# A set of fillers taken out of TensorE's instruction stream: threshold WARM from 0.8 to 0.0

## The chip, the core and the metric

The kernel runs on one core of a Trainium2 chip. The metric is the time of one execution on the device, in microseconds (us); the median of several executions is compared. Engines are written as in the profile: PE is TensorE (PEld its weight loads), DVE is VectorE, ACT is ScalarE, POOL is GpSimd, and SP issues most of the DMAs.

## What is computed

The input is x of 4 batches x 1024 tokens x 256 channels. Two layers follow, each with a layer norm ahead and a residual around it:

```python
x = x + attn(layernorm(x))        # theta, phi (64 wide), g (256): (theta phi^T / 16) g, no softmax
x = x + ffn(layernorm(x))
# ffn: h = rmsnorm(x); q, k, v = h @ wqkv.T    (16 heads, 4 kv heads, 16 wide), rope on q and k
#      x = x + softmax(causal(q k^T / 4)) v @ wo.T
#      h = rmsnorm(x); router: softmax(h @ gate_w.T), the best 2 of 8 experts per token
#      out = sum over the chosen experts of (silu(h w1^T) * (h w3^T)) w2^T * weight
```

## The kernel before

The first attention has no softmax, so the kernel forms it per batch as a 256 x 256 product ("gram", L2016, from the normalized tokens `xn`, then "square", L2029) and applies it to the tokens ("x1", L2038). "xnT" (L2009) and "hT" (L2045) are transposes of 128 x 128 tiles by TensorE. "k_mm", "q1_mm", "q2_mm" (L2071) and "v" (L2056) are the projections of the second attention; "max" (L2085, L2088, L2092, L2093) computes scores only for their row maxima, which DVE takes (L1881, L1883); "maxT" (L2098) transposes the maxima; "score" (L2105) computes the scores, ACT takes their exponential (L1360), POOL masks, and "pv" (L2119) multiplies with v. "wo" (L2126) closes a batch. The rows of each batch are then sorted by expert and go through "blockT", "up", "gatedT", "down" (L2139, L2152/L2167, L2174, L2189).

Nothing is ordered by hand. `plan()` simulates the five engines in Python, with an assumed duration for each step (`WORK_OF`), and writes out one fixed list of steps per engine. Each engine then works through its list in order, and waits for semaphores where a step needs another engine's result or a bank of PSUM (7 banks go around among the steps; the 8th is that of "pv").

The change touches one helper in this plan, `keep_warm(until)`. It is called whenever the planner is about to place a step on PE that starts at the planned time `until`. While the steps placed within the last `WINDOW` (3.4) us of planned time ahead of `until` add up to no more than `WARM` times `WINDOW`, and a planned gap is left, it puts a filler ("warm") into PE's list: one product of the 128 x 128 identity with itself, in f32, planned at `WARM_TOOK` (0.22 us), into a PSUM bank that is free in the plan. A filler's result is read by nobody. In the kernel it is

```python
if stage == "warm":
    q.wait_ge("load_eye", 16)
    e.matmul(bk[:, 0:P], ident, ident, start=True, stop=True)
```

Of the kernel before, what the change touches and what calls it, by code (L numbers as in the profile page):

```python
# [242 lines left out]
           "blockT", "up", "gatedT", "down")  # L243

WARM, WINDOW, WARM_TOOK, WARM_FROM = 0.8, 3.4, 0.22, 5.0

SPACING = 3.5

# [1984 lines left out]
```

## Time and profile before

| | us |
|---|---|
| median of three executions | 1090.14 |
| lowest, highest | 1088.01, 1091.58 |
| span of the profiled execution, first to last instruction | 1087.9 |
| TensorE busy in the span | 1042.4 |

### The profile page before, as it was taken

What the parts mean: (1) busy time and instruction counts of PE and PEld (TensorE: products, weight loads), DVE (VectorE), ACT (ScalarE), POOL (GpSimd) and SP (SyncE); (2) the same over time, 40 slices, a digit from 0 to 9 for tenths busy, and PEclk for the clock granted to TensorE, in tenths of its full rate; (3) what the DMA queues carried; (4) which work ended last, traced back from release to release, by engine and by line L of the source; (5) the groups of instructions that cost most, each with busy time, mean ns of one, the idle gap of its engine ahead of it and who ended that gap; (6) DMA issues with size and microseconds to landing.
All of it is one profiled execution on the core that took longest, in us unless ns stands there. A gap on an engine that the chain in (4) does not pass through costs nothing.

```text
span 1087.9 us, 19824 instructions
## 1 busy us (share of the span) xinstructions
PE 1042.4 (96%) x6630; PEld 619.5 (57%) x6630; DVE 763.2 (70%) x1811; ACT 581.1 (53%) x1124; POOL 421.9 (39%) x493
## 2 busy tenths in 40 slices
PE   7999999999999999999999999999999999999996
PEld 6765335564435333354333533456667986679996
DVE  4699999768788897788886699243485555555552
ACT  3563566646677887747666566641432244453320
POOL 2020232625643134521434512555637833344332
PEclk9999999999999999999999999999999999999999
DMA  6334113322324656723342511233434432222322
GB/s 192 124 94 122 51 49 106 93 76 77 100 75 140 187 175 193 216 78 99 105 126 85 140 55 37 65 75 74 103 83 98 99 62 38 45 36 40 50 43 27
DMA packets 85732, 101.50 MB, mean 93 GB/s; under 512 B 17632, under 2 KB 73312, under 8 KB 85632
## 3 DMA queue, kind: packets, MB, share of 16 engines
q1 hardware_dynamic: 70752, 80.60, 25.7%
q0 software_dynamic: 14880, 19.64, 9.5%
q8 instruction: 55, 0.90, 0.3%
q14 instruction: 45, 0.37, 0.1%
HBM read 55.76 MB, written 41.14 MB: 89 GB/s over the span
## 4 chain that ended last, share of the span: by engine, by line
PE 70%; DVE 19%; issue 4%; ACT 4%; POOL 1%; DMA 1%; SPq 0%; POOLq 0%; DVEq 0%; ACTq 0%
PE psum L2167 12%; PE psum L2189 9%; PE psum L2119 9%; PE psum L2152 8%; PE psum L2105 7%; DVE psum L1881 7%; PE psum L2085 4%; DVE mx L1883 3%; PE psum L2161 3%; PE psum L2071 3%; PE psum L2126 2%; PE psum L2088 2%; ACT probs_mem L1360 2%; PE psum L2092 2%; PE psum L2038 2%
## 5 line engine op out<-in xcount | busy, mean ns | idle before, releaser
L1360 ACT ACTIVATE probs_mem<-psum 128x512 f32<-128x512 f32 (+1 forms) x464 | 233.6, 585 | 103.3 <-PE psum L2105 98.6
L1881 DVE CUSTOM_DVE_ANT_1 psum<-psum,masking 128x640 f32<-128x640 f32 (+3 forms) x256 | 256.9, 1046 | 31.1 <-PE psum L2088 28.2
L2105 PE MATMUL psum<-stack_mem 98*128 98x512 bf16 (+3 forms) x768 | 170.9, 327 | 6.0 <-ACT probs_mem L1360 2.4
L1259 POOL DMA_INDIRECT out<-yout,labels x68 | 108.9, 1602 | 164.7 <-DVE yout L1961 78.1
L1200 POOL TENSOR_SCALAR_AFFINE_SELECT probs_mem<-probs_mem 128x512 f32<-128x512 f32 x104 | 67.7, 653 | 237.4 <-ACT probs_mem L1360 237.1
L2105 PEld LDWEIGHTS psum<-stack_mem 98*128 98x128 bf16 x768 | 65.0, 97 | 104.5 <-ACT probs_mem L1360 21.5
L1385 ACT ACTIVATE gated<-psum 128x512 f32<-128x512 f32 x68 | 40.6, 597 | 150.9 <-PE psum L2152 68.9
L2119 PE MATMUL psum<-probs_mem,v 128*17 128x512 f32 (+3 forms) x1152 | 116.0, 490 | 0.6 <-ACT heads_out L1367 0.2
L2189 PE MATMUL psum<-w_mem,gated 128*128 x480 | 114.4, 381 | 0.0
L1883 DVE TENSOR_REDUCE mx<-psum 128x4 f32<-128x512 f32 (+2 forms) x96 | 96.6, 1040 | 19.5 <-PE psum L2093 11.8
L2085 PE MATMUL psum<-stack_mem 96*128 96x512 bf16 x256 | 94.8, 383 | 8.6 <-DVE mx L1881 5.1
L2189 PEld LDWEIGHTS psum<-w_mem,gated 128*128 128x128 f32 x480 | 88.1, 190 | 24.6 <-issue 14.6
L1360 ACT ACTIVATE gated<-psum 128x512 f32<-128x512 f32 x144 | 78.9, 617 | 37.8 <-PE psum L2105 37.0
L2152 PE MATMUL psum<-w_mem,blockT 128*128 x200 | 95.2, 599 | 2.7 <-ACT probs_mem L1360 1.7
L1955 DVE TENSOR_TENSOR gated<-psum,gated 128x512 f32<-128x512 f32 x68 | 47.0, 692 | 48.2 <-PE psum L2167 20.6
L1951 DVE SCALAR_TENSOR_TENSOR gated<-gated,psum 128x512 f32<-128x512 f32 x68 | 46.6, 686 | 46.5 <-ACT gated L1385 45.0
L2088 PE MATMUL psum<-stack_mem 96*128 96x128 bf16 (+3 forms) x256 | 76.3, 298 | 0.0
L1230 POOL DMA_INDIRECT routed<-hrow,route_mem x64 | 64.1, 1002 | 29.2 <-DVE hrow L1940 16.1
L2167 PE MATMUL psum<-blockT,probs_mem 128*128 128x128 f32 x576 | 70.2, 275 | 0.0
L2167 PEld LDWEIGHTS psum<-blockT,probs_mem 128*128 128x128 f32 x576 | 68.6, 192 | 0.9
L2085 PEld LDWEIGHTS psum<-stack_mem 96*128 96x128 bf16 x256 | 24.7, 96 | 74.7 <-DVE mx L1881 33.5
L2167 PE MATMUL psum<-blockT,stack_mem 128*128 128x128 f32 x544 | 66.2, 275 | 0.0
(243 smaller groups left out, 1770.1 us busy)
## 6 DMA issues: line engine op xcount, KB each, us to landing
block<-routed SPq DMA_DIRECT2D x68, 129.0 KB
w_mem<-in_w13T SPq DMA_DIRECT2D x16, 512.0 KB, 4.4
qk_parts<-w_mem SPq DMA_DIRECT2D x16, 384.0 KB, 2.6
stack_mem<-qk_parts SPq DMA_DIRECT2D x32, 192.0 KB, 3.0
w_mem<-in_x SPq DMA_DIRECT2D x8, 512.0 KB, 5.3
out<-w_mem SPq DMA_DIRECT2D x8, 512.0 KB, 4.1
x_late<-out SPq DMA_DIRECT2D x8, 512.0 KB, 5.0
stack_mem<-qk_parts SPq DMA_DIRECT2D x32, 128.0 KB, 2.6
```

What stands on the lines that cost most here:

```text
L1200: e.affine_select(pb[:, :, q0:q0 + P], pb[:, :, q0:q0 + P], [[0, GRP], [1, P]], ALU.is_ge, 0.0, base=0, channel_multiplier=-1).then_inc(se ...
L1259: e.indirect_dma_start(out_rows, bass.IndirectOffsetOnAxis(ap=to, axis=0), youts[w % NYOUT], None, bounds_check=NBATCH * SEQ - 1, oob_is_e ...
L1360: e.activation(probs[probs_of(m)][:, hh:hh + n, q0:CH], grid(turn[step][0][:, 0:n * (CH - q0)], n), ACT.Exp, scale=float(HD) ** -0.5).then ...
L1881: e.tensor_tensor_reduce(keys, keys, masked(w), 1.0, -3e38, ALU.add, ALU.max, to).then_inc(sem["max"], 1)
L1883: e.tensor_reduce(to, took, AX.X, ALU.max).then_inc(sem["max"], 1)
L2085: e.matmul(bk[:, 0:CH], rows_of, s[0:STACK, 0, GRP, :], start=True, stop=True)
L2088: m = e.matmul(to, rows_of, s[0:STACK, r, GRP, 0:w], start=True, stop=True)
L2105: m = e.matmul(bk[:, i * (CH - q0):(i + 1) * (CH - q0)], s[0:STACK + NMAX, kt // TPR, GRP, kt % TPR * P:(kt % TPR + 1) * P], s[0:STACK + N ...
L2119: m = e.matmul(pv_bank[32 * hh:32 * hh + HD + 1, q0:CH], v1[:, b, kt, g, :], pb[:, hh, q0:CH], start=(kt == KEYS[r][0]), stop=(kt == KEYS[ ...
L2152: m = e.matmul(bk, blockT[w % 2][:, k], w13_s[:, k, bass.ds(offset[w] + half * FFN, FFN)], start=(k == 0), stop=(k == KD - 1))
L2167: m = e.matmul(bk[:, c * P:(c + 1) * P], slots[copies_of(w)[0] % NSLOT][:, k, half * FFN + c * P:half * FFN + (c + 1) * P], blockT[w % 2][ ...
L2189: m = e.matmul(bk[:, 0:D], rowsT[:, k * P:(k + 1) * P], w2_mem[:, bass.ds(offset[w] + k * D, D)], start=(k == 0), stop=(k == KF - 1))
```

## The change

`WARM` becomes 0.0. The loop of `keep_warm` then stops as soon as anything was placed within the last 3.4 us of planned time. It still adds a filler where nothing was.

```diff
-WARM, WINDOW, WARM_TOOK, WARM_FROM = 0.8, 3.4, 0.22, 5.0
+WARM, WINDOW, WARM_TOOK, WARM_FROM = 0.0, 3.4, 0.22, 5.0
```

PE's list has 87 fillers before and 8 after. The 79 that are gone stood: 12 of 15 ahead of the first batch's gram, 16 of 21 around the first hT (17, 1 and 3 before, 5 after), 10 of 10 in the second batch's projections, and 41 of 41 later (11 at 346 to 352 us, 1 at 438 us, 28 from 466 to 496 us, 1 at 628 us of the profiled execution). The order of all other steps is the same on all five engines; some waits for a bank now stand on the next step in the place of the filler.

The first place is PE's start. L2001 is the product of the weights theta and phi ("pair"), L1997 a filler, L2016 the gram of the first batch; the words in brackets are the semaphores that the instruction waits for.

```order
 L2001 MATMUL psum<-w_mem 128x256
 L1997 MATMUL psum<-ident 128x128 [waits load_eye]
-L1997 MATMUL psum<-ident 128x128 x3
-L1997 MATMUL psum<-ident 128x128 [waits pair_out]
-L1997 MATMUL psum<-ident 128x128 x10
+L1997 MATMUL psum<-ident 128x128 x2
 L2016 MATMUL psum<-w_mem 128x256 [waits xn]
```

The gram moves up by 12 fillers; its own waits for `xn` stay.

The second place is PE at the first batch's hT (L2045, which waits for `h` from ACT); L2071 is the projection for the keys, whose list of waits names `hT_out` (ACT's copy of the transposes).

```order
 L1997 MATMUL psum<-ident 128x128 [waits xnT_out]
-L1997 MATMUL psum<-ident 128x128 x14
+L1997 MATMUL psum<-ident 128x128 x2
 L2045 MATMUL psum<-ident,w_mem 128x128 [waits h]
 L2045 MATMUL psum<-ident,w_mem 128x128 x3
-L1997 MATMUL psum<-ident 128x128
 L2045 MATMUL psum<-ident,w_mem 128x128 [waits h,x1]
 L2045 MATMUL psum<-ident,w_mem 128x128 x3
-L1997 MATMUL psum<-ident 128x128 x3
 L2071 MATMUL psum<-w_mem 64x512 [waits wqkv,hT_out,x1]
```

Of the 17 fillers ahead of the transposes 5 stay (the piece shows the last three, two more stand ahead of it), and the one between the transposes and the three behind them go.

The third place is PE around 492 to 498 us of the trace: L2092 and L2093 end a pair of maxima, L2119 is pv.

```order
-L1997 MATMUL psum<-ident 128x128
-L1997 MATMUL psum<-ident 128x128 [waits max]
-L1997 MATMUL psum<-ident 128x128 x7
 L2119 MATMUL psum<-probs_mem,v 17x128 [waits mask]
 L2119 MATMUL psum<-probs_mem,v 17x128 x3
-L1997 MATMUL psum<-ident 128x128 [waits max]
-L1997 MATMUL psum<-ident 128x128 x2
 L2119 MATMUL psum<-probs_mem,v 17x512 [waits pv_out,mask]
 L2119 MATMUL psum<-probs_mem,v 17x512 x3
 L2119 MATMUL psum<-gated,v 17x512 x4
```

The two groups of pv move up to the end of the maxima; the nine and the three fillers ahead of them go.

## Rows read from the trace of the kernel before

**Rows 1.** Busy time of each engine over the span (the page's first part).

```profile
PE 1042.4 (96%) x6630; PEld 619.5 (57%) x6630; DVE 763.2 (70%) x1811; ACT 581.1 (53%) x1124; POOL 421.9 (39%) x493
```

**Rows 2.** All fillers of the kernel (groups by line: busy us, mean ns, idle before).

```profile
L1997 PE MATMUL psum<-ident 128*128 128x128 f32 x174 | 26.5, 297 | 0.1
```

**Rows 3.** Stretches: busy us (xcount) of PE, PEld, DVE, ACT, POOL, PEclk, DMA, GB/s.

```profile
60.00:105.00 45.00, 42.76 (x247) 29.79 (x247) 42.69 (x125) 24.64 (x48) 5.99 (x7) 1.00 0.43 130
466.00:496.00 30.00, 27.48 (x171) 18.18 (x172) 28.36 (x65) 12.08 (x34) 7.06 (x15) 1.00 0.23 67
540.00:1079.00 539.00, 532.25 (x3327) 356.15 (x3319) 319.12 (x683) 234.34 (x416) 243.61 (x275) 1.00 0.32 70
```

**Rows 4.** Timeline of PE, 7.9 to 22.4 us (start, us, engine, line, tiles).

```profile
7.94 2.07 PE L2001 MATMUL psum<-w_mem 64*128 64x256 f32 x4 [7.94 <-DMA w_mem<-in_wphi]
9.94 5.66 PE L1997 MATMUL psum<-ident 128*128 128x128 f32 x30
15.44 7.07 PE L2016 MATMUL psum<-w_mem 128*128 128x256 f32 x32
22.34 1.04 PE L2009 MATMUL psum<-ident,w_mem 128*128 128x128 f32 x8
```

**Rows 5.** Fillers by their source line, in 9 to 14 us and in 36 to 41 us.

```profile
L1997 PE MATMUL psum<-ident x19: 421/421/580, 9.9 to 13.9; 128*128 128x128 f32 x19
...
L1997 PE MATMUL psum<-ident x34: 275/275/343, 36.5 to 40.2; 128*128 128x128 f32 x34
```

**Rows 6.** Timeline of ACT, 10 to 16 us.

```profile
10.04 0.60 ACT L1270 ACTIVATE w_mem<-psum 128x512 f32<-128x512 f32 x1 [7.96 <-PE psum L2001]
10.54 2.07 ACT L1278 ACTIVATE w_mem<-w_mem,rt 128x256 f32<-128x256 f32 x4
12.96 2.08 ACT L1278 ACTIVATE w_mem<-w_mem,rt 128x256 f32<-128x256 f32 x4 [0.36 <-DVE rt L1458]
```

**Rows 7.** Chain that ended last, 9 to 31 us (start us, us, what).

```profile
10.01 5.59 PE psum L1997 x30
15.60 6.91 PE psum L2016 x32
...
30.61 0.69 DVE w_mem L1822
```

**Rows 8.** Timeline of PE, 36 to 44 us.

```profile
36.46 4.03 PE L1997 MATMUL psum<-ident 128*128 128x128 f32 x34
40.72 0.66 PE L2045 MATMUL psum<-ident,w_mem 128*128 128x128 f32 x4 [0.23 <-ACT w_mem L1285]
...
43.20 1.90 PE L2071 MATMUL psum<-w_mem 128*64 128x512 f32 x4
```

**Rows 9.** Timeline of PE where the next fillers stand, 71 to 76 us.

```profile
71.75 1.28 PE L1997 MATMUL psum<-ident 128*128 128x128 f32 x10
73.60 1.99 PE L2038 MATMUL psum<-w_mem 128*128 128x256 f32 x8 [0.57 <-ACT w_mem L1325]
```

**Rows 10.** Chain, 438 us: the one filler that it holds in mid-kernel.

```profile
438.35 0.42 PE psum L1997 x2
```

**Rows 11.** Timeline of PE, 492 to 500 us.

```profile
492.13 2.31 PE L1997 MATMUL psum<-ident 128*128 128x128 f32 x18
...
494.81 0.94 PE L1997 MATMUL psum<-ident 128*128 128x128 f32 x6
...
499.61 0.39 PE L2105 MATMUL psum<-stack_mem 98*128 98x512 bf16 x1 [0.72 <-ACT probs_mem L1360]
```

**Rows 12.** Timeline of ACT, 494 to 500 us.

```profile
495.87 3.31 ACT L1299 ACTIVATE hrow<-hrow,rstd 128x256 f32<-128x256 f32 x8 [0.42 <-DVE rstd L1444]
499.08 1.22 ACT L1360 ACTIVATE probs_mem<-psum 128x384 f32<-128x384 f32 x3
```

**Rows 13.** Stretches after PE's last matmul (columns as in rows 3).

```profile
1078.40:1082.40 4.00, 0.04 (x1) 0.00 (x0) 0.48 (x1) 0.00 (x0) 1.21 (x1) 1.00 0.24 27
1082.40:1083.00 0.60, 0.00 (x0) 0.00 (x0) 0.00 (x0) 0.00 (x0) 0.15 (x1) 0.69 0.00 0
```

## The prediction

> **What bounds the kernel now.** I read the page first. TensorE (PE) is busy 1042.4 us of the span of 1087.9 [rows 1], so whatever stands in PE's list and isn't needed is suspect. All fillers together are 174 records, two for each of 87, with 26.5 us of busy time [rows 2]. That is the most that their removal could be worth if PE never waited for another engine; it would be 2.4% of the span. So the question for each group of fillers is whether PE had something else to do in that time.
>
> The stretches of the span answer most of it [rows 3]. From 60 to 105 us DVE is busy 42.69 of 45 us, from 466 to 496 us 28.36 of 30. In both, and in the shorter one at 346 to 352 us, PE waits for DVE to empty banks, and the fillers fill that wait. From 540 us to PE's end PE is busy 532.25 of 539 us and DVE 319.12: there PE is the bound, but only one filler (at 628 us) stands there. What comes earlier in the kernel and is saved for good is therefore kept to the end, since that last stretch only moves.
>
> Then I read the start as a timeline and as the chain that ended last. PE begins with the pair product at 7.94 us, runs 15 fillers (30 records) from 9.94 to 15.44, and then the gram, 32 records from 15.44 to 22.34 [rows 4]. The chain of what ended last goes through these fillers and the gram, and on to DVE's first x1 at 30.61 us [rows 7]. So the fillers at the start are on the path. What the gram needs is ready earlier: ACT normalizes the first four tiles from 10.54 us on, at about 0.5 us each, and the other four from 12.96 us [rows 6].
>
> **The change, part by part.**
>
> *The first 12 fillers.* A record's median duration is 421 ns up to 13.9 us, and 275 ns in the group at 36 us [rows 5]: until about 14.2 us TensorE ran at its lower level (1.2 GHz), and then at 2.4 GHz, after some 6.3 us in which it had run without a pause since 7.94. From the starts, the 20 records before 14.26 took 0.216 us each ((14.26 - 9.94) / 20), and the last ten 0.118 (1.18 us to 15.44). The gram's records take (22.34 - 15.44) / 32 = 0.216 us each at the high level; at the low one I take twice that, 0.432. The pair product's records of as many columns took 0.50 ((9.94 - 7.94) / 4), which is my upper bound. In the changed kernel three fillers stay: 6 x 0.216 = 1.3 us, so the gram can start at 11.24. The first tile is there by then: 10.54 + 0.52 = 11.06, with some latency 11.3. While the clock is low a gram step (four records) takes 1.73 us and ACT delivers a tile every 0.5, the fifth at about 13.5, so `xn` is never late again. From 11.3 to 14.26 seven records run, the other 25 take 25 x 0.216 = 5.4 us, and the gram ends at 19.7 where it ended at 22.34: **2.65 us earlier**. With 0.50 us for a slow record it is 2.4. If the clock rises one microsecond later than before, this loses 0.5 us, so I hold 1.2 to 3.6 us for this term.
>
> After the gram come PE and ACT alone, then DVE at 30.61 with the x1 of the first batch. DVE's work ahead of that is done long before: in the chain it is PE that DVE waits for there [rows 7].
>
> *The 16 fillers around the first hT.* The 17 ran from 36.46 to 40.49 us, and the transposes then still waited 0.23 us for ACT's h; the keys' projection starts at 43.20 behind ACT's copy [rows 8]. Nothing that PE did there held anything up: **0 us**. But here the cover goes. Five fillers end about 1.2 us after 36.46, at 37.6, and PE then stands for 3.1 us until 40.72; of the 5.6 us to 43.20 it works only for the two groups of transposes. If TensorE's clock falls in there, the projections start at the low level. The only fall in this trace is at the end: after PE's last matmul at 1078.4 the granted clock is still 1.00 up to 1082.4 and 0.69 on the mean over the next 0.6 us [rows 13], so it fell some 4.2 us after the last work. That is longer than the 3.1 us without any work, and shorter than the 5.6 with a little. From the row alone I call it open, and take no fall.
>
> The Trainium skill, "TensorE: Matmul & The Clock Gate", section "Why this matters for your kernels", speaks against the change here: it warns that a gap in TensorE's work of about the length opened here, between bursts of matmuls, takes the clock back to half. By that rule the sum would be near zero (the first rival); by the row it is the 2.65 us.
>
> *The 10 fillers of the second batch.* The five from 71.75 us are followed by a wait of 0.57 us for ACT [rows 9], and those near 85 us stand in the stretch in which DVE is full [rows 3]: 0. PE then idles 1.9 us at the first, shorter than anything above.
>
> *The 41 later.* 39 lie in the stretches in which DVE is full: 0. The one at 438 us is in the chain with 0.42 us [rows 10], but some 20 us later PE waits for ACT and POOL anyhow, and the one at 628 us has a wait for DVE behind it: 0 to 0.4 us together, taken as 0. The largest group is the 9 and 3 fillers at 492 and 494.8 us (2.31 and 0.94 us) [rows 11]. Without them PE is 3.1 us ahead, since the masks of that pv are long done. But ACT, in order, first has the eight steps that wait for DVE's rstd until 495.87, and begins the exponentials only at 499.08 [rows 12]; PE waits for the first of them until 499.61 either way [rows 11]. DVE is without a gap ahead of rstd. So the lead turns into a wait of 3.8 us: 0 us, and a second place at which the clock may fall, of the same kind.
>
> **Sum.** 1087.9 - 2.65 = 1085.2 us of span. The median of the timed runs lies 2.2 us above the profiled span; I keep that: **1087.5 us**.
>
> **Rivals.**
>
> *The clock falls around the first hT and the gain is given back.* For: 5.6 us with PE nearly idle. Against: two groups of transposes break them, and the only row of a fall shows 4.2 us of no work at all. Price: the low level lasts, as at the start, some 6.3 us of running, here from 43.2 to 49.5, in which PE gets half as far: 3.1 us lost. These projections feed DVE (it waits for them), so it is on the path. Sum: 1090.14 - 2.65 + 3.1 = 1090.6; with a fall late in the gap or a quick return 1089.
>
> *Slower by over 0.3%: the clock stays low for long after that gap.* Each microsecond at the low level from 43.2 us on costs half a microsecond, and 2.65 us are in hand. It ends above 1093.4 only if the low level lasts more than (3.3 + 2.65) x 2 = 11.9 us; at 15 us it gives 1090.14 - 2.65 + 7.5 = 1095. Against: the clock came up after 6.3 us at the start, and PE runs almost without pause after 43.2.
>
> *The lead of PE at 495 us counts.* If the exponentials aren't what PE needs there, 3.1 us more are kept: 1090.14 - 2.65 - 3.1 = 1084.4. For: it is PE that bounds the rest. Against: the wait for ACT that stands in the row today.
>
> *The fillers at the start cost nothing* (something else holds the gram or its followers, a table or a weight that lands late): 1090.
>
> **How the numbers follow.** Gain at the start kept, 0.48: 1087.5, its own range 1085.5 to 1089. Clock falls at the first hT, 0.30: 1089 to 1091. No gain for another reason, 0.06. Clock low for long, 0.06: 1095. Lead at 495 us kept, 0.10: 1084.4. The range of 1084.5 to 1091.5 leaves out the long low clock and the lower half of the last case, and a little at either end. A measurement of this kernel tells about 0.3% (3.3 us) from no change, so faster starts below 1086.9. The likeliest case is 0.6 us short of that; the three runs of before lie within 3.6 us, so I give it about a third of the likeliest case (0.16) and nearly all of the lead (0.09): 0.25 faster. Slower has the long low clock and a small share of the short one: 0.08. The same: 0.67.
>
> **What would show it.** Right: the gram ends near 19.7 us, DVE's first x1 starts near 28.0, records behind 40 us keep 275 ns (128 columns), PE waits 3 us or more for ACT near 493 us, and the span is 2 to 3 us shorter. Wrong: a granted clock under 1.00, or projections of the first batch with doubled durations at 40 to 50 us; a clock that rises later than some 14 us at the start; a first x1 that is not earlier.

## The result and the profile after

The changed kernel takes 1094.39 us in the median of 8 executions (1092.34 to 1099.18), the kernel before 1089.2 in 8 (1087.93 to 1091.58). The ratio is 1.0049 (95% interval 1.0036 to 1.0063): some 5.3 us slower. The forecast was 1087.5 us with a range of 1084.5 to 1091.5: the time lies outside it, and the gain did not come. The profiled execution has a span of 1092.5 us, with TensorE busy for 1032.0 us (10.4 less than in [rows 1]) and a mean granted clock of 0.988 (0.998 before). So PE was busy 10 us less, and the kernel became slower.

The page of the changed kernel shows PE's busy share and the granted clock in 40 equal slices of the span, in tenths.

```profile
PE   7899899999998999988999999999999999999996
...
PEclk9899999999999999998999999999999999999999
```

The second slice (27 to 55 us) has a clock of 8 tenths. PE has five slices of 8 where the page of before has none. The timeline of PE shows the start and the first hT (start, us, line, tiles).

```profile
9.66 1.65 PE L1997 MATMUL psum<-ident 128*128 128x128 f32 x6
11.10 7.54 PE L2016 MATMUL psum<-w_mem 128*128 128x256 f32 x32
18.48 1.04 PE L2009 MATMUL psum<-ident,w_mem 128*128 128x128 f32 x8
...
32.59 1.35 PE L1997 MATMUL psum<-ident 128*128 128x128 f32 x10
36.85 2.16 PE L2045 MATMUL psum<-ident,w_mem 128*128 128x128 f32 x8 [2.91 <-ACT w_mem L1285]
39.74 5.31 PE L2071 MATMUL psum<-w_mem 128*64 128x512 f32 x8 [0.73 <-issue]
```

Three fillers (6 records) are left at 9.66 us, the gram runs from 11.10 to 18.48 us (15.44 to 22.34 in [rows 4]). Five fillers (10 records) stand at 32.59; then PE waits 2.91 us for ACT's h. The eight transpose records that follow take 2.16 us, and the eight of the keys' projection 5.31 us. In the kernel before such eight took 3.82:

```profile
43.20 3.82 PE L2071 MATMUL psum<-w_mem 128*64 128x512 f32 x8
```

These are the stretches around each fall of the clock in the changed kernel (columns as in [rows 3]).

```profile
32.60:35.90 3.30, 1.34 (x12) 1.15 (x10) 3.27 (x30) 1.04 (x3) 0.00 (x0) 1.00 0.71 240
36.00:42.70 6.70, 5.12 (x12) 2.18 (x12) 2.48 (x15) 6.48 (x14) 0.00 (x0) 0.50 0.60 190
42.80:46.00 3.20, 3.20 (x16) 1.93 (x16) 2.73 (x4) 0.75 (x2) 0.00 (x0) 1.00 0.89 282
...
349.00:353.30 4.30, 2.66 (x17) 0.68 (x17) 4.30 (x13) 3.79 (x10) 0.00 (x0) 1.00 0.59 164
353.40:356.70 3.30, 3.30 (x18) 0.58 (x11) 3.13 (x11) 0.47 (x2) 0.00 (x0) 0.50 1.13 339
...
466.00:469.40 3.40, 1.38 (x7) 0.50 (x7) 2.85 (x7) 3.40 (x9) 0.72 (x1) 1.00 0.52 133
469.50:472.80 3.30, 3.30 (x9) 1.67 (x9) 1.58 (x4) 2.74 (x7) 0.28 (x1) 0.50 0.13 41
496.50:500.10 3.60, 1.98 (x15) 0.60 (x7) 3.12 (x15) 2.69 (x7) 0.00 (x0) 1.00 0.14 29
500.20:506.90 6.70, 5.69 (x21) 1.85 (x22) 3.48 (x12) 5.49 (x14) 1.27 (x2) 0.50 0.65 174
```

The clock is granted at 0.50 (1.2 GHz) from 35.9 to 42.8 us, from 353.4 to 356.8, from 469.4 to 472.8 and from 500.1 to 507.0. Ahead of each, PE worked only part of the time: 1.34 of 3.30 us, 2.66 of 4.30, 1.38 of 3.40, 1.98 of 3.60. Each of the four is a place that had fillers before, and PE is busy during most of each low stretch, so it pays for it.

How DVE's lead went is read from its timeline at five steps, in the kernel before:

```profile
45.15 0.68 DVE L1842 TENSOR_TENSOR w_mem<-psum,w_mem 64x512 f32<-64x512 f32 x1 [2.31 <-PE psum L2071]
...
337.83 1.23 DVE L1883 TENSOR_REDUCE mx<-psum 128x2 f32<-128x1024 f32 x1 [0.32 <-PE psum L2093]
...
359.14 1.23 DVE L1881 CUSTOM_DVE_ANT_1 psum<-psum,masking 128x1024 f32<-128x1024 f32 x1
...
470.26 0.43 DVE L1905 TENSOR_TENSOR hrow<-psum,hrow 128x264 f32<-128x264 f32 x1
...
506.36 0.23 DVE L1932 COPY route_mem<-psum 128x64 f32<-128x64 f32 x1
```

and at the same steps in the changed kernel, with the first x1 ahead of them:

```profile
26.74 0.69 DVE L1822 TENSOR_TENSOR w_mem<-psum,w_mem 128x512 f32<-128x512 f32 x1 [4.24 <-PE psum L2038]
...
43.18 0.68 DVE L1842 TENSOR_TENSOR w_mem<-psum,w_mem 64x512 f32<-64x512 f32 x1 [4.22 <-PE psum L2071]
...
336.86 1.23 DVE L1883 TENSOR_REDUCE mx<-psum 128x2 f32<-128x1024 f32 x1 [0.32 <-PE psum L2093]
...
359.64 1.23 DVE L1881 CUSTOM_DVE_ANT_1 psum<-psum,masking 128x1024 f32<-128x1024 f32 x1 [1.55 <-PE psum L2088]
...
472.01 0.43 DVE L1905 TENSOR_TENSOR hrow<-psum,hrow 128x264 f32<-128x264 f32 x1 [0.98 <-PE psum L2126]
...
510.05 0.23 DVE L1932 COPY route_mem<-psum 128x64 f32<-128x64 f32 x1 [0.91 <-PE psum L2134]
```

The first x1 starts at 26.74 us where it was 30.61 [rows 7]: 3.87 us ahead. It is 1.97 ahead at the keys' projection (43.18 for 45.15), 0.97 ahead at a step before the second fall (336.86 for 337.83), 0.50 behind after the second fall (359.64 for 359.14), 1.75 behind after the third (472.01 for 470.26), 3.69 behind after the fourth (510.05 for 506.36), and the span is 4.6 us longer. The loss comes in steps, and each of the four falls has one: 1.90, 1.47, 1.25 and 1.94 us. Another 1.0 us goes between the first two falls, with no fall beside it. All of it goes at one place: PE waits 1.21 us for a DMA in the changed kernel, and the same step of the kernel before (at 117.75 us) has no wait for a DMA.

```profile
116.81 1.45 PE L2105 MATMUL psum<-stack_mem 98*128 98x512 bf16 x5 [1.21 <-DMA stack_mem<-mneg_parts]
```

The last 0.9 us (3.69 behind, then 4.6) are lost after 510 us, where the clock does not fall before PE's last matmul.

PE around 495 us, in the changed kernel:

```profile
493.65 0.41 PE L2119 MATMUL psum<-probs_mem,v 128*17 128x128 f32 x8
495.26 1.05 PE L2119 MATMUL psum<-probs_mem,v 128*17 128x512 f32 x8 [1.20 <-ACT heads_out L1367]
...
498.10 0.38 PE L2105 MATMUL psum<-stack_mem 98*128 98x512 bf16 x1
501.13 1.29 PE L2105 MATMUL psum<-stack_mem 98*128 98x512 bf16 x2 [2.66 <-ACT probs_mem L1360]
```

Without its twelve fillers PE doesn't run ahead: the second group of pv waits 1.20 us for ACT's copy of the first, and the scores wait 2.66 us for the exponentials, 3.86 us together.

### The profile page after: what moved, and what is told of

Its sections match the earlier page's. It is cut to its first block, busy times and chain, and to the rows that moved or that the text cites. A ratio compares the mean times of both kernels' runs of the same rounds, so it can differ in the third digit from the quotient of the medians.

```text
span 1092.5 us, 19511 instructions
## 1 busy us (share of the span) xinstructions
PE 1032.0 (94%) x6472; PEld 601.6 (55%) x6472; DVE 762.1 (70%) x1811; ACT 581.1 (53%) x1124; POOL 422.7 (39%) x493
## 4 chain that ended last, share of the span: by engine, by line
PE 64%; DVE 20%; DMA 6%; issue 5%; ACT 4%; POOL 1%; SPq 0%; POOLq 0%; DVEq 0%
PE psum L2119 9%; PE psum L2152 8%; PE psum L2167 8%; PE psum L2189 8%; DVE psum L1881 7%; PE psum L2105 7%; DMA out<-yout,labels 5%; PE psum L2085 4%; DVE mx L1883 3%; PE psum L2161 3%; PE psum L2071 3%; PE psum L2126 2%; ACT probs_mem L1360 2%; PE psum L2088 2%; PE psum L2038 2%
## 5 line engine op out<-in xcount | busy, mean ns | idle before, releaser
L2119 PE MATMUL psum<-probs_mem,v 128*17 128x512 f32 (+3 forms) x1152 | 117.3, 495 | 1.8 <-ACT heads_out L1367 1.4
L1883 DVE TENSOR_REDUCE mx<-psum 128x4 f32<-128x512 f32 (+2 forms) x96 | 96.5, 1040 | 19.5 <-PE psum L2093 14.3
L1961 DVE TENSOR_SCALAR yout<-psum,labels 128x256 f32<-128x256 f32 x68 | 32.8, 482 | 53.5 <-PE psum L2189 31.3
```

Of the source, the lines that this page charges most:

```text
L1883: e.tensor_reduce(to, took, AX.X, ALU.max).then_inc(sem["max"], 1)
L2119: m = e.matmul(pv_bank[32 * hh:32 * hh + HD + 1, q0:CH], v1[:, b, kt, g, :], pb[:, hh, q0:CH], start=(kt == KEYS[r][0]), stop=(kt == KEYS[ ...
```

## The experiments

Each kernel was timed in rounds beside the kernel before on the same chip. "At 0.997" counts the executions whose mean granted clock was 0.997 or more; the last column is the range of that mean. A low stretch of 7 us takes 0.003 off it. The fall behind PE's last matmul [rows 13] is in every mean. One execution of each kernel is profiled: the eight profiles with a mean of 0.997 or more (that of the kernel before among them) have no fall ahead of PE's last matmul, the nine with 0.995 or less have one to five. The kernel before itself was at 0.997 in 87 of the 121 executions beside these experiments: 14 of 19 beside e1 to e4, 16 of 29 beside e5, e6, e7 and e9, 23 of 29 beside e8, e10 and e11, 12 of 15 beside e12, and 22 of 29 beside e13 to e15.

| kernel | median us | before, us | ratio (95%) | at 0.997 | mean clock |
|---|---|---|---|---|---|
| changed kernel | 1094.39 | 1089.2 | 1.0049 (1.0036 to 1.0063) | 0 of 8 | 0.986 to 0.991 |
| e1_start: without the 12 | 1087.19 | 1090.25 | 0.9977 (0.9962 to 0.9992) | 5 of 7 | 0.995 to 0.998 |
| e2_hT: without the 16 | 1096.3 | 1090.25 | 1.0047 (1.0033 to 1.0062) | 0 of 5 | 0.990 to 0.993 |
| e3_346: without the 11 | 1091.58 | 1090.25 | 1.0012 (1.0 to 1.0023) | 3 of 12 | 0.994 to 0.997 |
| e4_466: without the 28 | 1094.72 | 1090.25 | 1.0048 (1.0033 to 1.0064) | 0 of 6 | 0.989 to 0.995 |
| e5_others: without the other 12 | 1088.63 | 1088.93 | 1.0 (0.9987 to 1.0012) | 10 of 12 | 0.994 to 0.998 |
| e6_transposes | 1090.71 | 1088.93 | 1.0016 (1.0002 to 1.003) | 5 of 12 | 0.994 to 0.998 |
| e7_half: without 14 of the 28 | 1091.61 | 1088.93 | 1.002 (1.0009 to 1.0031) | 2 of 12 | 0.993 to 0.997 |
| e9_start_kept | 1098.71 | 1088.93 | 1.0084 (1.0071 to 1.0097) | 0 of 6 | 0.984 to 0.987 |
| e8_early | 1086.78 | 1088.51 | 0.9983 (0.9973 to 0.9993) | 6 of 12 | 0.993 to 0.998 |
| e10_more | 1087.02 | 1088.51 | 0.9988 (0.9979 to 0.9996) | 11 of 11 | 0.997 to 0.998 |
| e11_hT_kept | 1090.06 | 1088.51 | 1.0017 (1.0005 to 1.003) | 0 of 12 | 0.986 to 0.995 |
| e12_early_more | 1090.34 | 1089.09 | 1.0011 (1.0002 to 1.002) | 2 of 11 | 0.991 to 0.997 |
| e13_250 | 1091.97 | 1091.3 | 1.0004 (0.9994 to 1.0014) | 10 of 12 | 0.996 to 0.998 |
| e14_early_250 | 1089.3 | 1091.3 | 0.9982 (0.9971 to 0.9994) | 7 of 12 | 0.995 to 0.997 |
| e15_hT_250 | 1095.6 | 1091.3 | 1.0034 (1.0022 to 1.0045) | 0 of 12 | 0.992 to 0.995 |

Gains and losses in us below are (ratio - 1) x 1090.

### One group at a time

Fillers were taken out of the finished plan of the kernel before, by their number in it, so that every other step stayed as it was:

```diff
+        gone = {*range(3, 15)}
+        orders["PE"] = [s for s in orders["PE"] if s[0] != "warm" or s[1] not in gone]
+        steps = [s for s in steps if s[0] != "warm" or s[1] not in gone]
```

**e1_start** is this diff: fillers 3 to 14, ahead of the first gram. (The added lines move all line numbers behind them: a filler is L2000 here, the gram L2019.)

> The kernel before without the 12 fillers ahead of the first gram; the other 67 that the change takes away stay. Clock theory (the fillers later in the list kept TensorE's clock up, and the change lost time because it fell at four places): no fall of the clock here, so the gain at the start stays to the end. The changed kernel had DVE's first x1 3.87 us earlier than before, of which some 0.4 us was there before the first matmul: 3 to 3.9 us faster than before. Rival (an early lead is lost in later waits anyhow): DVE's first x1 earlier by as much, and the whole within 1 us of before.

Measured: ratio 0.9977, 2.5 us faster. Its timeline of PE:

```profile
9.70 1.65 PE L2000 MATMUL psum<-ident 128*128 128x128 f32 x6
11.14 8.24 PE L2019 MATMUL psum<-w_mem 128*128 128x256 f32 x32
19.22 1.04 PE L2012 MATMUL psum<-ident,w_mem 128*128 128x128 f32 x8
```

The gram ends at 19.22 us, 3.1 us before that of [rows 4]; the mean clock over the profiled execution is 0.997, with no fall before PE's last matmul. The lead stays: the span of the profile is 1084.9 us, 3.0 shorter than before. The median's gain is a little under the 3 to 3.9 us of the clock theory, but the interval (0.9 to 4.1 us) takes in both that range and, just, the 1 us of the rival.

**e2_hT**: `gone = {*range(20, 36)}`, the 16 around the first hT.

> The kernel before without the 16 fillers around the first hT. Clock theory: the granted clock falls to 0.50 between 38 and 48 us and the keys' projection (8 records) takes 5.3 us and not 3.8; slower than before by about 1.9 us, what DVE's lead shrank by there in the changed kernel. Rival (the lead shrank there because of an issue or a wait, not the clock): the clock stays at 1.00, and the time is within 0.5 us of before or later by the same 1.9.

Measured: 1.0047, 5.1 us slower, more than either theory said. The clock did fall at the hT, from 41.9 to 48.7 us, and so later against the steps than in the changed kernel. There 0.9 us of the low stretch fell into PE's wait for ACT; here it covers the keys' projection almost from end to end:

```profile
43.21 6.51 PE L2074 MATMUL psum<-w_mem 128*64 128x512 f32 x8 [0.73 <-issue]
```

That is 6.51 us where the changed kernel took 5.31 and the kernel before 3.82. The profile had a second fall where no filler had been taken:

```profile
253.50:256.90 3.40, 2.32 (x23) 2.06 (x21) 3.33 (x6) 2.34 (x5) 3.18 (x4) 1.00 0.31 69
257.00:263.70 6.70, 6.04 (x28) 2.26 (x26) 3.95 (x5) 3.64 (x10) 2.24 (x2) 0.50 0.07 15
```

The kernel before has the same lull at the same steps, and the clock held there in its profile (the stretch that begins with the same four scores, 2.31 us of work in 3.4):

```profile
250.60:254.00 3.40, 2.31 (x21) 2.01 (x20) 3.33 (x6) 2.48 (x6) 3.18 (x4) 1.00 0.29 65
```

So the same stretch of instructions can end with a fall or without one. Its cause in e2 was open; e15 below takes it up.

**e3_346**: `gone = {*range(46, 57)}`, the 11 at 346 to 352 us.

> The kernel before without the 11 fillers at 346 to 352 us. Clock theory: the clock falls for 3.4 us or more near 350 to 360 us, 1.5 to 2 us slower than before, unless the fall depends on where the kernel's steps lie in the chip's own time, in which case some executions show it and others don't. Rival (fillers there are free to remove, as predicted): 0.

Measured: 1.0012, 1.3 us slower. Three of the twelve executions had a mean clock of 0.997 and a median of 1089.42 us, the nine others 0.995 or less and 1092.86. One program, two outcomes, 3.4 us apart, told apart by the clock: the "sometimes" of the expectation. The profile is one of the nine:

```profile
346.00:349.70 3.70, 2.43 (x12) 0.87 (x12) 3.59 (x13) 3.08 (x6) 0.63 (x1) 1.00 0.27 71
349.80:356.60 6.80, 6.59 (x31) 1.33 (x33) 6.77 (x19) 4.80 (x12) 0.00 (x0) 0.50 0.76 231
```

**e4_466**: `gone = {*range(58, 86)}`, the 28 at 466 to 496 us.

> The kernel before without the 28 fillers at 466 to 496 us. Clock theory: falls near 470 and near 500 us, 3 us slower (1.2 and 1.9 us of DVE's lead went at these places in the changed kernel). Rival (as predicted, PE's lead only becomes a wait): 0.

Measured: 1.0048, 5.2 us slower; no execution kept its clock. Falls at 486.4 and 500.0 us, the first elsewhere than in the changed kernel:

```profile
483.00:486.40 3.40, 1.59 (x7) 0.89 (x7) 3.32 (x8) 0.55 (x3) 0.72 (x1) 1.00 0.14 46
486.50:489.80 3.30, 3.30 (x21) 2.37 (x20) 2.75 (x8) 0.36 (x2) 0.53 (x1) 0.50 0.14 30
496.60:500.00 3.40, 1.00 (x5) 0.53 (x6) 2.73 (x12) 3.40 (x10) 0.15 (x1) 1.00 0.29 57
500.10:503.40 3.30, 3.30 (x16) 0.82 (x15) 1.25 (x3) 2.61 (x6) 1.02 (x2) 0.50 0.84 286
```

**e5_others**: `gone = {*range(36, 46), 57, 86}`. These are the ten in the second batch's projections and the ones at 438 and 628 us.

> The kernel before without the 12 fillers that the clock never seemed to need: 10 in the second batch's projections, those at 438 and 628 us. Both theories: the time of before within 1 us, 0.4 us faster at best. If the granted clock falls somewhere all the same, then small gaps matter too, and it is 1 to 3 us slower.

Measured: 1.0 (0.9987 to 1.0012), with 10 of 12 executions at 0.997: while the other fillers stand, taking these twelve out changes neither the clock nor the time by anything that shows.

**e9_start_kept** is the changed kernel with its first 12 put back: `gone = {*range(20, 87)}`.

> The changed kernel with its 12 fillers ahead of the first gram put back. If the parts add up, it is slower than the changed kernel by what these 12 cost alone (2.5 us): ratio to before 1.0072, 7.8 us slower than before. If the single costs of the three later groups simply add, 5.1 + 1.3 + 5.2 = 11.6 us slower than before.

Measured: 1.0084, 9.2 us slower than before, between the two sums. The start's 12 are worth 3.8 us against the changed kernel (1.0084 - 1.0049; the two intervals leave room for 2.5), and the later groups together cost less than the sum of their single costs (11.6 us). The profile has five falls ahead of PE's last matmul, at 42.4, 100.4, 353.0, 492.9 and 506.6 us. The one at 100.4 us lies behind the ten fillers of the second batch, which are gone here too, and DVE falls 1.2 us further back there. So the ten are not without use in every kernel, though e5 by itself shows none.

**e11_hT_kept** is the changed kernel with the 16 around the hT put back: `gone = {*range(3, 15), *range(36, 87)}`.

> The changed kernel with its 16 fillers around the first hT put back. If they alone are worth what their absence cost the kernel before, it is 5 us faster than the changed kernel: about the time of before, ratio 1.000. By DVE's lead in the changed kernel alone, which shrank by 1.9 us there, 2 us faster than the changed kernel: ratio 1.003. No fall of the clock before 340 us in either case.

Measured: 1.0017. Against the changed kernel these 16 give back (1.0049 - 1.0017) x 1090 = 3.5 us: between the 2 us of DVE's lead and the 5 us of e2. As expected the profile has no fall ahead of 340 us; it has two, at 485.1 and 498.7 us, and none at 346 to 352 us, whose fillers are gone as well.

### How much filling, and of what kind

**e7_half**: `gone = {*range(59, 86, 2)}`.

> The kernel before without every second one of the 28 fillers at 466 to 496 us (14 go). Clock theory: with half of the fillers the stretch of PE without work before the exponentials is some 1.6 us longer, not 3 to 4, so the clock holds in most executions: within 1.5 us of before. If only the full set holds it: 5 us slower, as without all 28. Rival without a clock: half of what all 28 cost, 2.6 us.

Measured: 1.002, 2.2 us slower; 2 of 12 executions at 0.997. The time alone fits the rival's 2.6 us too. The clocks speak against it: 10 of 12 executions were at 0.996 or less, where the kernel before had 13 of 29 beside it. So half of the fillers do not hold the clock in most executions, as the clock theory had expected. The one profile has a single fall, from 469.1 to 472.5 us, where e4 had two.

**e6_transposes**: in the branch of "warm",

```diff
+                    if 20 <= at[0] < 36:
+                        e.transpose(bk[:, 0:P], ident, ident)
+                    else:
-                    e.matmul(bk[:, 0:P], ident, ident, start=True, stop=True)
+                        e.matmul(bk[:, 0:P], ident, ident, start=True, stop=True)
```

> The kernel before with all 87 fillers, but the 16 around the first hT are transposes of the identity by TensorE in the place of plain products: the same count, tile, place and length of work. If the clock theory holds and a transpose counts as work like any other, nothing changes (within 1 us of before, no fall near 40 us). If a transpose does not hold the clock up, as the Trainium skill has it, the granted clock falls near 40 us and the time is that of the kernel without these 16, about 5 us slower than before. If what the missing fillers cost is not the clock but something in the list, this kernel is like before in any case and shows no fall.

Measured: 1.0016 (1.7 us), 5 of 12 executions at 0.997. The expectation had one thing wrong, as the timeline shows:

```profile
35.52 1.35 PE L2003 MATMUL psum<-ident 128*128 128x128 f32 x10
36.71 1.47 PE L2001 MATMUL psum<-ident 128*128 128x128 f32 x12
39.78 0.66 PE L2051 MATMUL psum<-ident,w_mem 128*128 128x128 f32 x4 [1.60 <-ACT w_mem L1288]
```

Twelve transposes are 12 records in 1.47 us, where twelve products are 24 in twice that: a transpose of this tile shows as one record, and PE was left with a wait of 1.60 us. So it was not the same length of work. Still, without any of the 16 no execution of 5 was at 0.997 (e2), and with half the work as transposes 5 of 12 were (16 of 29 of the kernel before beside it); the profile has a mean clock of 0.998 and no fall near 40 us. Transposes do something for the clock. Whether as much as products of the same length was not measured. The Trainium skill, "TensorE: Matmul & The Clock Gate", section "Part 4: PE-mode transpose", says that they don't count as work in the same way; these runs don't decide it.

**e8_early**, with `gone = {*range(6, 15)}` and

```diff
+            q.wait_ge("set", 1)
+            for _ in range(14):
+                e.matmul(bank[6][:, 0:P], pad[:, 0:P], pad[:, 0:P], start=True, stop=True)
             for step in orders["PE"]:
```

> The kernel before with 14 fillers more at its very start (products of a cleared 128 x 128 tile, about 6 us of TensorE at the low clock, while it waits for the first weights until 7.9 us), and only 6 of the 15 ahead of the first gram. Clock theory: the clock is up by about 8 us in the place of 12 to 15, so the pair product and the gram run at the high level: the gram ends near 18.2 us (22.3 before, 18.5 and 19.2 without the 12 fillers), some 4 us faster than before and 1 to 1.5 faster than the kernel that only leaves the 12 out. If products of a cleared tile don't raise the clock, or if it comes up only after the loads, nothing is won over that kernel: 2.5 us faster than before.

Measured: 0.9983. The profile shows what was meant:

```profile
1.18 5.51 PE L1994 MATMUL psum<-left_rows 128*128 128x128 f32 x28 [1.18 <-POOL left_rows L1151]
7.83 1.13 PE L2007 MATMUL psum<-w_mem 64*128 64x256 f32 x4 [1.14 <-DMA w_mem<-in_wphi]
8.89 1.60 PE L2003 MATMUL psum<-ident 128*128 128x128 f32 x12
10.93 7.17 PE L2022 MATMUL psum<-w_mem 128*128 128x256 f32 x32 [0.43 <-ACT w_mem L1281]
17.94 1.04 PE L2015 MATMUL psum<-ident,w_mem 128*128 128x128 f32 x8
```

The 28 records run from 1.18 us; the pair product then takes 1.13 us (2.07 in [rows 4]) and the gram ends at 17.94. Products of a cleared tile raise the clock. Yet the ratio is no better than e1's, and not the 4 us that were expected: half of the executions had a mean clock of 0.995 or less (1087.5 us in the median), the other half 0.997 or more (1085.3).

**e10_more**: WARM at 1.0, and at most 3 fillers ahead of the first gram.

> WARM raised to 1.0 in the place of 0.0, and no more than 3 fillers ahead of the first gram: 14 more fillers than the kernel before has in its other places. The kernel before shows a mean clock under 0.996 in a third of its executions. If those are falls at stalls that its 72 other fillers don't quite cover, fewer executions show one here, and the median is 3 us under before, 0.5 better than the kernel without the 12 alone; if fillers by now stand in the way of work, it is slower than that kernel by up to 14 x 0.24 = 3.3 us.

Measured: 0.9988 (0.9979 to 0.9996); all 11 executions at 0.997 or more, where the kernel before had 34 of 121 at 0.996 or less. With more fillers no execution shows a fall. But the median is 1.3 us under before and not 3, and not below e1's; whether the added fillers stand in the way of work somewhere was not measured.

**e12_early_more** joins e8 and e10.

> Both together: the 14 early products and 6 fillers ahead of the gram, and WARM at 1.0 for all other places. The executions of the kernel with the early products alone were 1085.3 us in the median where the mean clock was 0.997 or above, and 1087.5 where it was 0.995 or below (6 of 12 each); those with WARM at 1.0 showed none below 0.997. If the falls are what the larger threshold prevents, hardly any execution shows one and the median is 1085.3 (ratio 0.9965 to 0.997). If the early products bring falls of their own, half of the executions stay slow, 1086.8.

Measured: 1.0011, slower than before, and the expectation failed. Only 2 of 11 executions were at 0.997. Why this kernel is slower than either of its parts is open. Its profile has one fall, at 251.3 us, in the lull that e2 had shown, where the plan has no filler even at a threshold of 1.0:

```profile
251.40:258.00 6.60, 5.90 (x27) 2.19 (x26) 3.89 (x5) 3.62 (x10) 2.17 (x2) 0.50 0.07 15
```

### The lull at 250 us

The three last kernels have 8 fillers more, 4 ahead of the product at 252.3 us and 4 ahead of the maxima at 256.2, in banks that ACT has emptied by then:

```diff
+        for at, bank_n, ahead in ((("v", 2, 1), 5, 300), (("max", 1, 0, 0, 2), 0, 310)):
+            more = [("warm", ahead + i) for i in range(4)]
+            for todo in (orders["PE"], steps):
+                todo[todo.index(at):todo.index(at)] = more
+            place.update(dict.fromkeys(more, (bank_n, 1)))
```

**e13_250** is the kernel before with them.

> The kernel before with all its fillers and 8 more where the planner saw no gap: 4 ahead of the product at 252.3 us that waits 1.1 us for DVE, 4 in the wait of 1.2 us ahead of the maxima at 256.2 us, into banks that ACT has emptied. If the falls that the kernel before shows in a third of its executions begin there, fewer executions have a mean clock of 0.996 or less, and the median is some 0.3 us lower; the fastest stay at 1088. If they begin elsewhere, nothing changes. If the fillers are in the way, 1 to 2 us slower throughout.

Measured: 1.0004 (0.9994 to 1.0014). 10 of 12 executions at 0.997 and none below 0.996; beside it the kernel before had 7 of 29 at 0.996 or less. Too few to tell, and no gain in time.

**e15_hT_250**: e2 with them.

> The kernel before without the 16 fillers around the first hT, with the 8 at 252 to 256 us. Without the 8 it was 5.1 us slower than before, and its profile showed two falls, 1.9 to 2.8 us of DVE's time at the hT and 2.2 at 257 us. If the second is a lull of its own that the 8 cover, what stays is the fall at the hT: 2.5 to 3 us slower than before (ratio 1.0025). If the missing 16 cost 5 us in some other way, the ratio stays at 1.0047.

Measured: 1.0034 (1.0022 to 1.0045), 3.7 us slower; e2 was 5.1. The profile has one fall in all of the kernel, at the hT; the second row is everything after it up to PE's end:

```profile
41.40:48.10 6.70, 5.84 (x10) 2.13 (x11) 2.02 (x8) 5.00 (x10) 0.00 (x0) 0.50 0.69 201
48.20:1080.00 1031.80, 1004.08 (x6427) 586.24 (x6427) 734.44 (x1661) 562.00 (x1085) 411.42 (x470) 1.00 0.35 91
```

Half of the 12 executions have a mean clock of 0.992 or 0.993, under the 0.994 of the profiled one, and so probably fall more than once. The six others have a median of 1094.65 us, 3.35 over the kernel before. The fall at the hT is thus worth 3 to 4 us when it lands as in this profile (the keys' projection takes 6.16 us), and the rest of e2's 5.1 us fits the second fall; the intervals of the two ratios (1.0033 to 1.0062 and 1.0022 to 1.0045) overlap, so that share is not settled.

**e14_early_250**: e8 with them.

> The kernel with the 14 early products and 6 fillers ahead of the gram, with the same 8 fillers at 252 to 256 us. Half of the executions of the kernel without these 8 had a mean clock of 0.995 or less (1087.5 us) and half of 0.997 or more (1085.3). If the falls are those at 250 us, seen in the profiles of two other kernels, most executions are at 1085.3 and the ratio to before is 0.9965 to 0.997. Otherwise it stays at 0.9983.

Measured: 0.9982 (0.9971 to 0.9994), where e8 had 0.9983, and 7 of 12 at 0.997 where it had 6. The lull at 250 us is not what divides e8's executions into two kinds.

## Why the prediction was wrong

**The fillers at the start: right, and a little more than forecast.** Predicted 2.65 us, 1.2 to 3.6. The gram ended at 18.48 us and DVE's first x1 came 3.87 us earlier, against 19.7 and about 28.0 forecast. The part beyond 2.65 is a first load that landed 0.28 us earlier and a clock that came up about two microseconds sooner in that execution (at 12.0 us for 14.3). Alone the step is worth 2.5 us (e1) or, in the changed kernel, 3.8 (e9 against it), both with intervals of 1.6 us or more to either side.

**The 16 fillers around the first hT: the step that failed.** The term was "0 us". The prediction saw the wait of 3.1 us (2.91 came), said "I call it open, and take no fall", and gave the fall 0.30 as a rival. It fell in every profile without these fillers (the changed kernel, e2, e9, e15) and in no profile with them, and no execution of e2 or e15 (17) had its clock at 0.997. The reading behind the choice was [rows 13]: at the kernel's end the clock fell some 4.2 us after the last matmul, and 3.1 is less. In the changed kernel it fell at 35.9 us, 2.0 us after the last filler and before the wait was over; in e2 and e15 it fell 4.3 and 3.8 us after the last filler, when the transposes were running again. One row of a fall gives one distance, and the distance is not a constant. The rule of the Trainium skill that the prediction quoted against itself got the outcome right: the clock went to half. It speaks of a gap, though, and 2.0 us into the wait the gap was not yet of the length that the rule and the prediction speak of. The size of the rival was about right: 3.1 us forecast, 3.5 to 3.7 by e11 and e15, but 1.9 of DVE's lead in the one profile of the changed kernel. How much a fall costs depends on what lies under the low stretch.

**The later groups: the same failure, and missed as a group.** For the fillers at 346 to 352 us the prediction wrote 0 and no clock at all; they cost 1.3 us, 3.4 in each execution that falls (e3). For those at 466 to 496 us it wrote "0 us, and a second place at which the clock may fall", without a price; they cost 5.2 us (e4). That DVE is full there [rows 3] was right and beside the point. With DVE as the bound PE works only part of the time ahead of each of these falls (2.66 of 4.30 us, 1.38 of 3.40, 1.98 of 3.60), and the low clock then lasts into stretches in which PE or ACT behind PE is the bound (at 500 to 507 us PE is busy 5.69 of 6.70 us at half speed).

**The lead at 495 us**: right as to its end in a wait (3.8 us forecast; 1.20 and 2.66 measured). The reason it gave was only half of it, since the second pv waits for ACT's copy as well.

**The other twelve**: 0, right as long as the other fillers stand (e5); e9 has a fall behind ten of them.

**The sum.** Start 2.5 us faster, hT 3.5 to 5.1 slower, 346 us 1.3, 466 us 5.2: 7.5 to 9.1 us slower where 5.3 was measured. Why the single prices add to more than the whole is not shown; an execution can fall in the lull at 250 us or elsewhere in any of these kernels, and a wait made longer by one fall may absorb part of the next. Of DVE's lead 1.0 us went into a wait for a DMA at 116.8 us, which the sum of the prediction did not have; why that transfer was the last to arrive there is open. So is where the clock falls in half of e8's executions, since its one profile had no fall. The rival on the slower side asked for one long low stretch of 11.9 us; what came was four short ones, some 20 us in all.

## What to carry to other kernels

In this kernel fillers on TensorE cost nothing that shows where another engine is the bound, and most of their own time ahead of work that is ready (e1): remove those ahead of ready work, keep those in stalls. Before taking one away, look not at what PE did in the stall but at what it does in the microseconds behind it, since that is what runs at half speed. And count the mean granted clock over many executions, not the falls in one profile: it told two outcomes of one program apart here (1089.4 and 1092.9 us), and showed that the kernel before falls too, in some three of ten executions (34 of 121).

## What the runs showed of the hardware

- TensorE's clock fell while PE still had work in pieces: with 1.34 of 3.30 us busy ahead of 35.9 us, 1.59 of 3.40 ahead of 486.4 (e4), and 2.32 of 3.40 ahead of 256.9 (e2), where its longest wait was 1.1 us.
